# Four graph layers on one core: transposes of split logits at full width, the own logit as an activation's bias, the last projection in three single-pass parts, and reordered work lists

## The reference

```python
def _L3_gnn_ref(X, A, W, a):                       # W: 256 x 128, a: 2 x 128 x 1
    h = jnp.einsum('bnf,fo->bno', X, W)
    att_self = jnp.einsum('bno,od->bnd', h, a[0])  # own logit, one per node
    att_neigh = jnp.einsum('bno,od->bnd', h, a[1]) # neighbour's logit, one per node
    e = att_self + jnp.swapaxes(att_neigh, 1, 2)
    e = jax.nn.leaky_relu(e, ALPHA)
    e = e + NEG * (1.0 - adj)[None, :, :]
    alpha = jax.nn.softmax(e, axis=-1)
    out = jnp.einsum('bij,bjo->bio', alpha, h)
    return jnp.concatenate([out, h], axis=-1)
...
h = jnp.maximum(_layernorm(x, axis=-1), 0.0)
x = x + _L3_gnn_ref(h, adj, L3_gnn_W, L3_gnn_a)
```

## Time and profile before

| | us |
|---|---|
| median of 3 runs | 2636.43 (2636.19 to 2638.84) |
| the profiled execution, its own time | 2638.98 |
| its span in the profile | 2637.1 |
| TensorE busy in the span | 2550.9 |
| VectorE busy | 2215.3 |
| ScalarE busy | 2078.0 |
| GpSimd busy | 1298.0 |

### The profile page before, as it was taken

How to read it: one execution, slowest core, us unless ns; L and a number is a source line. 1 busy time by engine, 2 the same in 40 slices (tenths; PEclk the granted TensorE clock), 3 DMA queues, 4 the chain that set the end, 5 groups by cost and what they waited for, 6 DMA issues and landing times.

```text
span 2637.1 us, 64646 instructions
## 1 busy us (share of the span) xinstructions
PE 2550.9 (97%) x21825; PEld 2333.0 (88%) x21825; DVE 2215.3 (84%) x8352; ACT 2078.0 (79%) x5708; POOL 1298.0 (49%) x2276
## 2 busy tenths in 40 slices
PE   4899999999999999999999999999999999999985
PEld 3789999999999999999999999999999999999874
DVE  5688888888888888888888888888888888888874
ACT  3788888888888888888888888888888888888852
POOL 4545455455455455455455455455545545545431
PEclk8999999999999999999999999999999999999996
DMA  4000000000000000000000000000000000000000
GB/s 129 5 2 9 18 18 10 18 17 10 17 18 14 14 17 18 10 18 18 9 18 17 10 18 18 10 18 17 10 17 18 10 18 18 12 15 14 9 9 13
DMA packets 41288, 44.32 MB, mean 17 GB/s; under 512 B 2816, under 2 KB 40448, under 8 KB 40832
## 3 DMA queue, kind: packets, MB, share of 16 engines
q1 hardware_dynamic: 40816, 39.14, 4.7%
q10 hardware_dynamic: 144, 1.05, 0.1%
HBM read 23.40 MB, written 16.78 MB: 15 GB/s over the span
## 4 chain that ended last, share of the span: by engine, by line
PE 93%; DVE 2%; ACT 0%; issue 0%; POOL 0%; DVEq 0%; ACTq 0%; POOLq 0%
PE pA L1116 15%; PE pB L1223 14%; PE pB L1116 10%; PE pB L1190 9%; PE pE L1116 7%; PE pC L1116 7%; PE pF L1347 4%; PE pF L1116 3%; PE pF L1360 2%; PE pE L1425 2%; PE pA L1334 2%; PE pE L1107 2%; PE pA L1183 2%; PE pC L1269 2%; PE pE L1410 1%; PE pE L1448 1%
## 5 line engine op out<-in xcount | busy, mean ns | idle before, releaser
L1223 PE MATMUL pB<-wout_high,B_h_high 128*128 128x258 f32 x1024 | 324.4, 317 | 1.5 <-POOL B_h_low L490 0.8
L704 ACT ACTIVATE F_s_t<-F_s_t,F_m 128x128 f32<-128x128 f32 x1024 | 324.7, 393 | 0.0
L1223 PE MATMUL pB<-wout_high,B_h_low 128*128 128x258 f32 x1024 | 290.4, 284 | 0.0
L1223 PE MATMUL pB<-wout_low,B_h_high 128*128 128x258 f32 x1024 | 289.7, 283 | 0.0
L1190 PE MATMUL pB<-probs,whs 128*128 128x128 f32 x2048 | 278.3, 279 | 1.8 <-DVE F_m L889 0.7
L1190 PEld LDWEIGHTS pB<-probs,whs 128*128 128x128 f32 x2048 | 250.2, 192 | 4.2 <-issue 3.7
L1116 PE MATMUL pA<-wh_high,A_hT_high 128*128 128x512 f32 x512 | 225.7, 441 | 5.3 <-POOL wh_low L398 5.3
L606 ACT ACTIVATE probs<-probs,A_m 128x128 f32<-128x128 f32 x512 | 199.4, 397 | 26.9 <-DVE A_m L889 26.9
L442 POOL TENSOR_TENSOR E_f<-E_h_t,F_zeros 128x4 bf16<-128x4 f32 x64 | 12.9, 202 | 408.4 <-ACT E_h_t L726 408.4
L1116 PE MATMUL pA<-wh_low,A_hT_high 128*128 128x512 f32 x512 | 203.6, 398 | 0.0
L1223 PEld LDWEIGHTS pB<-wout_high,B_h_high 128*128 128x128 f32 x1024 | 195.1, 190 | 8.8 <-POOL B_h_low L490 1.8
(11 more groups left out here) (270 smaller groups left out, 9946.4 us busy)
## 6 DMA issues: line engine op xcount, KB each, us to landing
xs<-in_x SPq DMA_DIRECT2D x64, 256.0 KB, 2.7
out_x<-xs SPq DMA_DIRECT2D x64, 256.0 KB, 2.1
probs<-in_a_heads ACTq DMA_DIRECT2D x1, 1024.0 KB, 5.1
F_pT<-in_w_heads SPq DMA_DIRECT2D x2, 512.0 KB, 6.9
xs<-in_w_out SPq DMA_DIRECT2D x1, 1024.0 KB, 9.6
F_s_t<-in_wijT SPq DMA_DIRECT2D x1, 512.0 KB, 5.8
C_h_t<-in_a_out SPq DMA_DIRECT2D x1, 256.0 KB, 9.9
D_q_t<-in_w SPq DMA_DIRECT2D x1, 256.0 KB, 7.2
```

What stands on the lines that cost most here:

```text
L704: last = act.activation(F_s_t[:, s, h, :], F_s_t[:, s, h, :], ACT.Exp, scale=-1.0, bias=F_m[:, s, h:h + 1])
L1223: last = pe.matmul(pB[:, 0, 0:D + 2], a, w[:, k, :], start=(k == 0 and i == 0), stop=(k == KH - 1 and i == 2))
```

## The change

It has five parts.

- The three tiles of split parts (`C_f3`, `E_f3`, `F_f3`) become 128 columns wide, set to zero once at the start, and are transposed whole. DVE copies the same rows as before.
- `both_logits` becomes `neighbours_logits`: of the two matmuls for each graph the one for the own logit goes. The own logit enters as the bias of the leaky relu on ACT, which is a value for each partition, so each graph needs an instruction of its own: two of 128x128 instead of one of 128x256, for C and for E. `pick` has two slices instead of four.
- The last projection `E_h` is made in three fp32r parts. `w3` gets a high and a low copy on DVE at the start (two more instructions in `w3_dots`). The transposed tile goes to the buffers `E_hT` that the residual layer's projection `E_m` uses: `E_hT3` writes the high part, and a new DVE step `E_low3` makes the low part. `E_low` now counts twice for each pair, and `E_m.0` and `E_h` wait accordingly.
- `E_h3T` and the tile of `w3_w` go. `wo_w` is loaded into `F_s_t`, `w3_w` into `E_h_t`.
- All four lists are new. Each is written from another starting point of the round, which by itself changes nothing. Seen from the same point: on TensorE `E_m.0` and `F_pTa.0` come just ahead of `B_wh0.0`, `C_ffn`, `A_pT.0` and `A_s.1` go from before `E_h` to after `B_wh0.1`, `D_q` goes from after `B_wh0.1` to after `B_wh3.1`, `E_s` and `A_f` change places, `E_zT` goes ahead of `C_pT`, and `F_o` follows `F_rT`, which follows `E_zT3`; `F_fT` goes up to a place between `F_pTa.1` and `A_s.0`. On ACT `A_fround` comes after `E_leaky` and `A_attn.1`; on DVE `F_x2`, `A_moments.0`, `C_g.1`, both `C_x1` and both `E_stats` now lie between `E_fTc` and `E_max.0`, and `D_stats.0`, three `moments` and `A_frest` between `E_max.0` and `E_max.1`.

The core of the diff:

```diff
-B_wh0.0:3 E_m.0:7 F_pTa.0:6 B_wh1.0:3 B_wh2.0:3 F_pTb.0:6 D_zT:5 B_wh3.0:3 E_m.1:7 C_hT:4 B_ol.1:3 D_k:5 F_pTb.1:6
-E_am:7 A_s.0:2 F_pTa.1:6 C_hid:4 D_v:5 F_fT:6 F_o:6 A_wh_hi.1:2 E_zT3:7 F_rT:6 B_oh.1:3 C_ffn:4 A_pT.0:2 A_s.1:2 E_h:7
-B_wh0.1:3 D_q:5 B_wh1.1:3 A_zT:1 E_fT:7 B_wh2.1:3 B_wh3.1:3 F_out:6 A_f:1 A_pT.1:2 E_s:7 B_ol.0:2 C_fT:3 F_s:5 C_s:3
-E_pT:7 A_wh_lo.0:1 E_o:7 B_oh.0:2 A_wh_hi.0:1 C_pT:3 E_zT:6 A_wh_lo.1:1 C_o:3
+B_wh0.1:3 A_s.1:2 C_ffn:4 A_pT.0:2 B_wh1.1:3 F_out:6 A_zT:1 E_fT:7 B_wh2.1:3 B_wh3.1:3 D_q:5 A_pT.1:2 E_s:7 A_f:1
+B_ol.0:2 C_fT:3 F_s:5 C_s:3 E_pT:7 A_wh_lo.0:1 E_o:7 B_oh.0:2 A_wh_hi.0:1 E_zT:6 C_pT:3 A_wh_lo.1:1 C_o:3 F_pTa.0:5
+E_m.0:6 B_wh0.0:2 B_wh1.0:2 F_pTb.0:5 B_wh2.0:2 B_wh3.0:2 E_m.1:6 F_pTb.1:5 D_zT:4 C_hT:3 B_ol.1:2 E_am:6 D_k:4
+F_pTa.1:5 F_fT:5 A_s.0:1 C_hid:3 D_v:4 E_zT3:6 F_rT:5 F_o:5 A_wh_hi.1:1 B_oh.1:2 E_h:6
...
-        C_f3, C_frest_t, C_fT_t = sb("C_f3", [P, 3 * 2 * G], BF16), sb("C_frest_t", [P, 2 * G]), sb("C_fT_t", [P, P], BF16)
+        C_f3, C_frest_t, C_fT_t = sb("C_f3", [P, P], BF16), sb("C_frest_t", [P, 2 * G]), sb("C_fT_t", [P, P], BF16)
...
-            for t in (C_fT_t, E_fT_t, F_fT_t):
+            for t in (C_f3, E_f3, F_f3, C_fT_t, E_fT_t, F_fT_t):
...
-            def leaky(chain, scores, slope):
+            def leaky(chain, scores, own, slope):
                 def step(p):
                     done(act, chain + "_s", p)
-                    act.activation(scores, scores, ACT.Prelu, alpha=slope).then_inc(S[chain + "_leaky"], 1)
+                    for s in range(G):
+                        one = scores[:, s * P:(s + 1) * P]
+                        last = act.activation(one, one, ACT.Prelu, bias=own[:, s, :], alpha=slope)
+                    last.then_inc(S[chain + "_leaky"], 1)
...
-                "E_hT3": copy("E_zT3", "E_hT3", E_h3T[:, :], pE[:, :], ACT.Relu), "E_hc": E_hc,
+                "E_hT3": copy("E_zT3", "E_hT3", E_hT[0][:, :], pE[:, :], ACT.Relu), "E_hc": E_hc,
...
+                dve.tensor_copy(w3_hl[0][:, :, :], w3_w[:, :, :]).then_inc(dots_made, 1)
+                dve.wait_ge(dots_made, BIASES - 1)
+                dve.tensor_tensor(w3_hl[1][:, :, :], w3_w[:, :, :], w3_hl[0][:, :, :].bitcast(F32), ALU.subtract)\
+                   .then_inc(dots_made, 1)
...
+                "E_x3": E_x3, "E_low3": relu_low("E_hT3", "E_low", E_hT, pE[:, :]),
...
-                n = f3.shape[1]
-                return pe.transpose(dst[0:n, 0:P // 2].bitcast(BF16), f3[:, :], ident_bf[:, :])
-            def both_logits(dst, fT):
+                return pe.transpose(dst[:, 0:P // 2].bitcast(BF16), f3[:, :], ident_bf[:, :])
+            def neighbours_logits(dst, fT):
                 for s in range(G):
-                    one = dst[:, s * P:(s + 1) * P]
-                    pe.matmul(one, fT[:, :], pick[:, 2 * s, :], start=True, stop=False)
-                    last = pe.matmul(one, pick[:, 2 * s + 1, :], fT[:, :], start=False, stop=True)
+                    last = pe.matmul(dst[:, s * P:(s + 1) * P], pick[:, s, :], fT[:, :], start=True, stop=True)
...
             def E_h(p):
-                done(pe, "E_hT3", p)
+                pe.wait_ge(S["E_low"], ELOW_OPS * (p + 1))
                 for s in range(G):
-                    for k in range(K):
-                        last = pe.matmul(pE[:, s * (F3 + 2):(s + 1) * (F3 + 2)], E_h3T[:, k * W + s * P:k * W + (s + 1) * P],
-                                         w3_w[:, k, :], start=(k == 0), stop=(k == K - 1))
+                    last = split_project(pE[:, s * (F3 + 2):(s + 1) * (F3 + 2)], E_hT, s, w3_hl)
```

## The result

The changed kernel takes 2653.13 us (median of 3 runs, 2653.09 to 2653.67) against 2636.43 before: a ratio of 1.0061, 95% interval 1.0038 to 1.0084. The forecast was 2624, faster; it came out slower, outside the 2609 to 2639 that the forecast gave itself and inside the 2588 to 2660 that takes in most of its rivals. The profiled execution took 2653.09, with a span of 2651.2, 14.1 more than before.

What follows compares the result with a forecast made beforehand. TensorE's instruction costs in a row were taken as the bound. Terms of -0.52, -0.22, +0.41, -0.1 and +0.2 gave -0.23 us a round, x 59 = -14, with the ends -12: 2624 us, range 2609 to 2639.

Steps and rivals of the forecast that it cites:

- new lists alone (`F_o` behind `F_rT`): `F_o`, in 32-column tiles, now follows `F_rT` and should wait some 0.11 us a round for an empty array.
- wide transposes and logits, without the wait: Full-width `E_fT`, `C_fT`, `F_fT` save TensorE time; `C_s` and `E_s` lose two of four matmuls each, -0.22 us a round.
- wait at `E_pT`: TensorE waits at `E_pT` because `E_max.1` stands late in DVE's list: +0.2 us a round, bounds 0 and +0.7.
- `E_h` in fp32r, with its seams: `E_h` as 12 fp32r matmuls at 0.108 us, +0.41 a round, with -0.1 for fewer plain-fp32-to-fp32r seams.
- its -0.52 for the transposes: Gain a round from full-width `E_fT` (0.24), `C_fT` (0.18) and `F_fT` (0.10, net of `F_o`'s wait); bounds 0 and -0.85.
- Its -0.1 for the seams: First fp32r matmul behind plain fp32 costs 0.20, not 0.12; two of five seams go, one may come: -0.1 us a round.
- `E_h` goes from 8 instructions at 0.111, 0.89 us: Starting price of the projection `E_h`; against it 12 fp32r matmuls at 0.108, 1.30 us, so +0.41 a round.
- `E_low3` and the second leaky relu lie open, some 1 us for each of the last four pairs; against that stand fewer matmuls: While the pipeline empties, added steps lie uncovered, partly offset; the term taken was +2 us, bounds 0 and +4.
- Rival (1): Logits queue behind DVE's work: `E_pT` waits 0.7 instead of 0.2, +0.27 us a round, 2654 us; chance 0.19.
- rival (4): A bf16 transpose empties the array at any width: the 0.52 is lost, +0.29 us a round, 2656 us; chance 0.08.
- Rival (2): `E_h` costs by columns: -0.16 instead of +0.41, so -0.80 us a round, 2591 us; chance 0.13.
- rival (3): `E_h` falls back to plain fp32's price: +1.77, so +1.13 us a round, 2705 us; chance 0.06.

Runs made afterwards that it cites:

- e4: The kernel before with the four new lists alone, without `E_low3`: 2650.36 us, ratio 1.0048.
- e3: The changed kernel, new lists kept, with `E_h` back as 8 plain fp32 instructions and without `E_low3`: 2616.92 us, ratio 0.9921.
- e5: The changed kernel with `E_max.1` moved directly behind `E_max.0` in VectorE's list: 2636.00 us, ratio 0.9994.
- e1: The kernel before with only the wide transposes and the own logit as bias; old lists and plain fp32 `E_h` stay: 2611.38 us, ratio 0.9898.
- e10: The changed kernel with the old lists, `E_low3` behind `A_norm.0`, three steps later than behind `F_rTc`: 2649.84 us, one run.
- e6: The changed kernel with the 12 fp32r matmuls of `E_h` cut from 130 to 66 moving columns: 2647.37 us, one run.
- e7: The changed kernel with 8 fp32r matmuls in `E_h` instead of 12, high part times low weights left out: 2620.52 us, one run.
- e9: The changed kernel with plain fp32 `E_h` and with `E_max.1` directly behind `E_max.0`: 2603.89 us, ratio 0.9872.
- e2: The changed kernel with the four lists of the kernel before, `E_low3` put behind `F_rTc` in VectorE's list: 2892.94 us, ratio 1.0973.

## Why the prediction was wrong

**The round.** Pairs of kernels give each term by itself:

| term | predicted | measured | by |
|---|---|---|---|
| new lists alone (`F_o` behind `F_rT`) | +0.11 | +0.12 | e4 - before |
| wide transposes and logits, without the wait | -0.85 | -0.79 | e3 - e4, less the wait |
| wait at `E_pT` | +0.2 | +0.25 | after - e5 |
| `E_h` in fp32r, with its seams | +0.31 | +0.45 | after - e3 |
| sum | -0.23 | +0.03 (the round: +0.04) | |

(The prediction had `F_o`'s 0.11 inside its -0.52 for the transposes; it is taken out here. Its -0.1 for the seams stands wholly in the line of `E_h`, though a seam behind `C_o` that it counts belongs to the lists. The pairs make a chain, so that the measured column adds up to the round proves nothing by itself.) In the round no term has the wrong sign, and the places were the right ones: time is lost ahead of and behind narrow transposes, the 12 matmuls go at 0.112, `E_max.1` is late. (That the array empties at the narrow tiles, and that the load sets the 0.112, are readings that fit.) But terms of half a microsecond with both signs were summed to a rest of 0.23, and three of the four were mis-sized, by 0.05 to 0.14, every time to the worse. In the second line the miss is `C_fT`, which gained 0.09 and not 0.18 (e1); the rest there nearly evens out. The largest miss is the step "`E_h` goes from 8 instructions at 0.111, 0.89 us". The earlier trace rows say otherwise: `E_h` starts at 1337.60 and the next product at 1338.41, which is 0.81. The missing 0.08 is the late second matmul of that product, and I counted just this again as a seam that goes. Without the double count, and with 12 matmuls at 0.112 and 0.03 more for the first of them, the term would have been 1.37 - 0.81 = +0.56, and +0.46 with the seams: what was measured. That would have turned the sum of the round from -0.23 to -0.08. In 59 rounds the misses of the table are 0.27 x 59 = 16 us.

**The ends.** The step "`E_low3` and the second leaky relu lie open, some 1 us for each of the last four pairs; against that stand fewer matmuls" was short by 10 us, and two things have no term in it at all: the new lists, and TensorE's clock. By pairs of kernels, the wide transposes and the bias take 2.8 us off the emptying (e1 - before), the new lists add 5.3 (e3 - e1; 3.0 by after - e10), and the fp32r `E_h` with `E_low3` adds 9.6 (after - e3). In the emptying, the E chains of the last pairs run one behind the other through the bank `pE`, and little covers them. The last pair, first in the kernel before, then in the changed one (TensorE: `E_zT3`, the start of `E_h`, `E_fT`):

```profile
2623.10 1.11 PE L1107 MATMUL pE<-ident,E_z_t 128*128 128x128 f32 x4 [3.81 <-DVE E_z_t L854]
2624.91 2.10 PE L1425 MATMUL pE<-w_w,E_h3T 128*128 128x130 f32 x8 [0.69 <-ACT E_h3T L573]
```

```profile
2635.70 1.11 PE L1115 MATMUL pE<-ident,E_z_t 128*128 128x128 f32 x4 [3.62 <-DVE E_z_t L862]
2638.23 0.47 PE L1124 MATMUL pE<-w_high,E_hT_high 128*128 128x130 f32 x1 [1.41 <-DVE E_hT_low L877]
2638.50 0.41 PE L1124 MATMUL pE<-w_low,E_hT_high 128*128 128x130 f32 x1
2638.72 0.41 PE L1124 MATMUL pE<-w_high,E_hT_low 128*128 128x130 f32 x1
```

From `E_zT3` to `E_h` 2.53 instead of 1.81: 0.72 for `E_low3`. From `E_h` to `E_fT` 4.42 instead of 3.69: 0.73 for 12 matmuls in the place of 8; they follow each other here at 0.21, not 0.112, since TensorE runs at 1.2 GHz, the lower of its two clocks (granted 0.50):

```profile
2634.00:2643.00 9.00, 4.22 (x17) 3.45 (x17) 1.46 (x4) 0.98 (x2) 2.01 (x7) 0.50 0.00 0
```

That is 1.45 for a pair and not 1, with more matmuls in `E_h` instead of fewer. But these two steps aren't the whole: from `E_fT` to `E_fT` the last pair takes 29.25 us after and 29.09 before, while 11.3 of the 12.1 us arise at the three pairs ahead of it, whose granted clock is 0.85, 0.84 and 0.66 instead of 0.94, 0.87 and 0.77. The low clock makes every product longer. The granted clock over the last 97 us of the span, before and after (last column but two):

```profile
2540.00:2637.00 97.00, 61.40 (x428) 48.16 (x420) 51.84 (x192) 32.89 (x91) 20.86 (x49) 0.74 0.03 12
```

```profile
2554.00:2651.00 97.00, 61.34 (x369) 47.19 (x369) 47.30 (x182) 31.52 (x91) 18.09 (x42) 0.67 0.03 11
```

With `E_low3` (after, e5, e6, e7, e10) it is 0.67 to 0.71, with a plain `E_h` (before, e1, e3, e4, e9) 0.72 to 0.80. What that costs shows in the last five pairs, from the sixth-last `E_fT` to the last: the changed kernel, e3, and e9, in which the work is e3's (the first figure behind the length is TensorE's busy time):

```profile
2481.18:2642.65 161.47, 121.91 (x907) 101.69 (x906) 102.04 (x379) 73.54 (x205) 48.58 (x98) 0.79 0.03 9
2454.86:2607.11 152.25, 112.17 (x888) 93.25 (x886) 99.38 (x374) 73.65 (x205) 48.55 (x98) 0.86 0.03 10
2439.07:2595.79 156.72, 117.18 (x888) 97.02 (x886) 99.29 (x374) 73.27 (x205) 48.46 (x98) 0.82 0.03 9
```

Against e3 the changed kernel is 9.2 longer, and TensorE's busy time is 9.7 longer: in total it doesn't wait more, it is busy longer. Some twenty more matmuls at 0.11 to 0.21 are 2.2 to 4.3 of that (an estimate from the paces above); the rest goes with the clock. e9 shows the clock's part alone: as many matmuls as e3, 5.0 more busy time, granted 0.82 instead of 0.86.

e5 and e6 empty in 197.6, the changed kernel in 200.6, though neither edit is meant to shorten that stretch, and e9 needs 4.3 more than e3. Executions of one kernel differ in the same way: the four of e9 range from 2602.67 us at a mean granted clock of 0.988 to 2606.20, the profiled one, at 0.984. So some 3 to 4 us of any emptying hang on where the clock happens to drop. Whether `E_low3` brings the lower clock with it or only coincides with it, and what sets where it drops, is open; no run here tells it apart. It wasn't tried either to start `E_h` with its high parts ahead of `E_low3`, since `E_low3` still reads the bank that `E_h` writes.

**Both together:** 16 + 10 = 26 of the 29 us between 2624 and 2653; the rest is that the profiled execution of before lay 2.5 above its median (the two traces differ by 14.1 us, the medians by 16.7).

**The rivals.** Rival (1) forecast 2654 and rival (4) 2656, close to what came, and both are wrong: the wait is 0.25, not 0.7, and the wide transpose does flow. A time that fits is no evidence for the mechanism; the distances at the places named were. Rival (2) is excluded by e6, rival (3) by the 0.112. The slower load of the Trainium skill ("TensorE: Matmul & The Clock Gate", section LDWEIGHTS), by which the wide transposes would have lost some 0.3 a round, an estimate, doesn't show: the next product starts 0.03 behind them.

## What to carry to other kernels

Count what an instruction costs from its start to the start of the next different one, and count each seam once. When gains and costs of similar size remain from a sum, the sign isn't known to better than the errors added up: here the rest of the change was worth 0.8% (e3), and one edit in it cost all of that and more, so price, and measure, each edit by itself. Three fp32r parts replace two plain fp32 instructions at a loss when the moving side is so narrow that an instruction costs the same 0.11 us either way, as here at 66 and 130 columns. And ask of the stretches where the pipeline fills or empties at which clock they run: a price read in the steady rounds was nearly doubled there.

## What the runs showed of the hardware that I had not expected

- An fp32r matmul with its own load of 128 columns takes 0.112 us at 66 and at 130 moving columns, a plain fp32 instruction 0.111, and at 258 columns it is 0.120: from 66 to 258 columns the price hardly changes.
- A bf16 transpose of 12 columns costs 0.33 us between full-width neighbours and one of 128 columns 0.11: from the first of four plain transposes to the next product it is 0.68 and 0.46, and 0.35 with nothing between the earlier trace rows.
- One step of VectorE that waits 1.44 us at a bad place lengthened most rounds by 5 us (e2): TensorE stood still for 1.83 us, and in 30 of 35 rounds its granted clock then fell to 0.50 for a while, which cost 3.1 us more. Three places later none of it is left (e10).
- A wait of 0.25 us on TensorE in each round leaves its busy share at 97%: of the page's figures only the chain, which fell from 93% to 79% TensorE, told of it (it is back at 93% in e5). It doesn't always: e1 has a wait of 0.2 at the same step, and its chain stays at 93%.
